# Early-fusion block: y hats clipped by ScalarE's int32 output, and attention scores as int16 in key-pair order

## The reference, cut to what matters

```
sampled = v00*(1-wy)*(1-wx) + v01*(1-wy)*wx + v10*wy*(1-wx) + v11*wy*wx

attn  = clip(round(q.k * sc / s), -128, 127)            # an integer times s
x_int = attn - max(attn);  x_int = max(x_int, 30*x0_int) # x0_int = floor(-0.6931/s)
qq    = floor(x_int / x0_int);  r = x_int - x0_int*qq
exp   = max(floor((r*(r + b_int) + c_int) * 2**(30 - qq)), 0)
ratio = round(sum(exp) / max(exp, 1))                    # rounded to a power of two
```

## Time and profile before

| what | value |
|---|---|
| median of 3 runs (lowest to highest) | 1015.75 us (1015.71 to 1016.1) |
| span of the profiled execution, first to last instruction | 1014.5 us |
| own time of the profiled execution | not given apart; the runs' median is 1.25 us above its span |
| PE busy | 880.8 us, 87% |
| DVE busy | 876.0 us, 86% |
| ACT busy | 779.8 us, 77% |
| POOL busy | 266.9 us, 26% |
| PE weight loads | 539.9 us, 53% |
| share of the 16 DMA engines | 24.5% |
| TensorE's granted clock, mean | 0.951 of full |

### The profile page before, as it was taken

The page is one execution under the profiler, slowest core; times in us unless marked ns, Lnnn a source line. Parts: engine busy times, 40 slices in busy tenths (PEclk is TensorE's granted clock), DMA queues, the critical chain, the costliest instruction groups (busy, mean ns, idle before and its releaser), DMA issues. The chain is left out here.

```text
span 1014.5 us, 18281 instructions
## 1 busy us (share of the span) xinstructions
PE 880.8 (87%) x5594; PEld 539.9 (53%) x5594; DVE 876.0 (86%) x1695; ACT 779.8 (77%) x1529; POOL 266.9 (26%) x248
## 2 busy tenths in 40 slices
PE   3568779999999999999999999999999999885757
PEld 1244436555565656565565656565556556453435
DVE  3964899998999899999999999999999999995960
ACT  2435587979888797979798988889797978785753
POOL 5210312315132313223041323141321414222120
PEclk9987769999999999999999999999999999998678
DMA  5110132221222232222213232323232232223030
GB/s 130 67 37 7 49 55 51 43 58 43 58 56 52 55 58 63 55 58 43 64 38 58 60 53 65 53 58 57 63 47 54 48 59 36 52 50 61 15 65 12
DMA packets 132628, 53.42 MB, mean 53 GB/s; under 512 B 105103, under 2 KB 131413, under 8 KB 132437
## 3 DMA queue, kind: packets, MB, share of 16 engines
q1 hardware_dynamic: 132532, 52.26, 24.5%
HBM read 19.75 MB, written 6.24 MB: 26 GB/s over the span
## 5 line engine op out<-in xcount | busy, mean ns | idle before, releaser
L563 POOL TENSOR_TENSOR ee_sb<-ee_sb,rs_sb 128x1020 f32<-128x1020 f32 x64 | 157.2, 2464 | 379.1 <-DVE rs_sb L1059 379.1
L1195 PE MATMUL bank<-hats_sb,ht_sb 127*96 127x400 f32 (+1 forms) x384 | 147.9, 522 | 1.7 <-DVE hats_sb L921 1.7
L1327 PE MATMUL bank<-w_out_sb,ge_sb 128*102 128x192 f32 x768 | 138.8, 331 | 10.9 <-DVE y_sb L1096 6.9
L1327 PEld LDWEIGHTS bank<-w_out_sb,ge_sb 128*102 128x102 f32 x768 | 120.3, 168 | 31.6 <-issue 17.8
L921 DVE TENSOR_TENSOR hats_sb<-hats_sb 126x1600 f32<-126x1600 f32 x64 | 127.2, 1987 | 0.7
L648 ACT ACTIVATE hats_sb<-bank 126x400 f32<-126x400 f32 (+1 forms) x256 | 108.2, 523 | 0.3 <-PE bank L1181 0.3
L727 ACT ACTIVATE a_sb<-scores,sc_sb 128x1020 f16<-128x1020 f32 x64 | 71.1, 1111 | 39.2 <-PE scores L1279 39.2
L1195 PEld LDWEIGHTS bank<-hats_sb,ht_sb 127*96 127x96 f32 (+1 forms) x384 | 58.7, 166 | 72.6 <-issue 69.3
L734 ACT ACTIVATE sq_sb<-rm_sb,sc_sb 128x1020 f32<-128x1020 f16 x64 | 73.5, 1148 | 18.2 <-DVE rm_sb L1031 18.0
L572 POOL TENSOR_TENSOR xshift_sb<-mv_sb,xshift_sb 102x4 f32<-102x4 f32 (+1 forms) x33 | 11.0, 333 | 279.9 <-DVE ve_sb L961 278.5
L1242 PE MATMUL bank<-xt_sb,w_in_sb 128*128 128x408 f32 (+1 forms) x204 | 82.0, 527 | 1.0 <-ACT xt_sb L667 1.0
(11 more groups left out here) (168 smaller groups left out, 1862.7 us busy)
## 6 DMA issues: line engine op xcount, KB each, us to landing
xc_sb<-x_col SPq DMA_DIRECT2D x32, 165.4 KB, 3.2
out<-y_sb SPq DMA_DIRECT2D x32, 153.0 KB
xa_sb<-txt SPq DMA_DIRECT2D x16, 231.0 KB
xr_sb<-txt SPq DMA_DIRECT2D x16, 231.0 KB
q_sb<-qb_sb SPq DMA_DIRECT2D x192, 12.8 KB, 1.9
samp_sb<-samp_sb SPq DMA_DIRECT2D x48, 50.0 KB, 1.9
tok_scratch<-tokb_sb SPq DMA_DIRECT2D x16, 75.0 KB
xa_sb<-tok_scratch SPq DMA_DIRECT2D x16, 75.0 KB
```

The costliest lines, as they stand in the source:

```text
L563: nc.gpsimd.tensor_tensor(EE[b][:], EE[b][:], RS[b][:].unsqueeze(2).to_broadcast([128, RT, TOK]), ALU.mult).then_inc(scaled_done, 1)
L1195: last = mm(dst, HT[0:rows, t.i, j, :], HATS[t.i][0:rows, 1 + j, :], start=(j == 0 and not odd), stop=(j == NCH - 2 and odd == 1))
L1327: last = mm(bank[t.banks[0]][0:TOK, 0:D], GE[:, f, t.i * TOK:(t.i + 1) * TOK], WOUT[:, f, :], start=(f == 0), stop=(f == FT - 1))
```

## The change

Two parts that share no data.

The y hats: ScalarE now writes the absolute y distance as int32, scaled by 2^31, so that every distance above 1 lands on the largest integer (`ONE_Y`); the x distance is scaled by 2^-31. `HAT` on DVE covers only the 400 x values, and `HATW` is a `scalar_tensor_tensor` that adds -2^31 to the integer y values and multiplies by x. `HAT` no longer waits for the y values; `HATW` does.

The scores: `A16`, `MX`, `M16`, `GQ` and `RM` become int16. PE writes the scores, and all softmax tiles up to `EE` keep them, in the order key pair, block, key of the pair (51 x 10 x 2). A new DVE stage `CLP` clips `A16` in place before `MAX`; `BND` is gone; `DST` becomes a plain `tensor_tensor` that subtracts the minimum less a lift from int16 values, so that results above 32767 stop there; the constants of `QQ`, `QQG`, `EP` and the square are changed to fit; `MX` and `RS` hold every value twice. Sums and the last minimum read by block across the key pairs, and ScalarE's Exp turns the order back to block, key.

```diff
-pe.LN2X.18 dve.MXB.53 act.LOG.15 dve.MAX.52 act.FFA.16 pe.HTT.5 dve.MXC.53 act.PR.15 dve.PREP0.0
-pe.SC.13 dve.MXB.52 act.FFN0.16 dve.DST.53 act.FFN1.16 pe.OFF.4 dve.BND.53 act.FFN2.16 sp.YO0.20
+pe.LN2X.18 dve.MXB.53 act.LOG.15 dve.CLP.52 dve.MAX.52 act.FFA.16 pe.HTT.5 dve.MXC.53 act.PR.15 dve.PREP0.0
+pe.SC.13 dve.MXB.52 act.FFN0.16 dve.DST.53 act.FFN1.16 pe.OFF.4 act.FFN2.16 sp.YO0.20
...
-                nc.scalar.activation(HATS[t.i][0:rows, 0, :], bank[t.banks[0]][0:rows, 0:SMP], ACT.Abs).then_inc(ax_done, 1)
+                nc.scalar.activation(HATS[t.i][0:rows, 0, :], bank[t.banks[0]][0:rows, 0:SMP], ACT.Abs,
+                                     scale=1.0 / ONE_Y).then_inc(ax_done, 1)
...
-                    nc.scalar.activation(HATS[t.i][0:rows, 1 + j, :], bank[t.banks[1]][0:rows, 0:SMP], ACT.Abs,
-                                         bias=float(-line)).then_inc(ay_done, 1)
+                    nc.scalar.activation(HATS[t.i][0:rows, 1 + j, :].bitcast(i32), bank[t.banks[1]][0:rows, 0:SMP], ACT.Abs,
+                                         scale=ONE_Y, bias=-line * ONE_Y).then_inc(ay_done, 1)
...
-                v.tensor_scalar(hat, hat, -1.0, 0.0, ALU.add, ALU.min).then_inc(hat_done, 1)
+                v.tensor_scalar(hat, hat, -1.0 / ONE_Y, 0.0, ALU.add, ALU.min).then_inc(hat_done, 1)   # hat: 400 columns, was 2000
...
-                v.tensor_tensor(hat[:, 1:, :], hat[:, 1:, :], hat[:, 0:1, :].to_broadcast([rows, NCH, SMP]),
-                                ALU.mult).then_inc(w_done, 1)
+                dve.wait_ge(ay_done, t.count(NCH, NCH))
+                v.scalar_tensor_tensor(hat[:, 1:, :], hat[:, 1:, :].bitcast(i32), -ONE_Y,
+                                       hat[:, 0:1, :].to_broadcast([rows, NCH, SMP]), ALU.add, ALU.mult).then_inc(w_done, 1)
...
-                nc.scalar.activation(A16[b][:].rearrange("p (j r) k -> p j (r k)", j=2), SCORES[:, :, 0:RC // 2], ACT.Identity,
-                                     scale=sc[:, SCORE:SCORE + 1], bias=MAGIC16).then_inc(a16_done, 1)
+                nc.scalar.activation(A16[b][:].rearrange("p (k j q) -> p j k q", j=2, q=RT),
+                                     SCORES[:, :, 0:RC // 2].rearrange("p j (k q) -> p j k q", q=RT), ACT.Identity,
+                                     scale=sc[:, SCORE:SCORE + 1], bias=EVEN_LIFT).then_inc(a16_done, 1)
...
-                nc.scalar.activation(RR[:], EE[b][:].rearrange("p h k -> p (h k)"), ACT.Exp, scale=-1.0).then_inc(rr_done, 1)
+                nc.scalar.activation(RR[:].rearrange("p (r k e) -> p r k e", k=KP, e=2), by_row(EE[b][:]), ACT.Exp,
+                                     scale=-1.0).then_inc(rr_done, 1)
...
+            def clip(t):
+                a = A16[t.i % 2][:]
+                dve.wait_ge(a16_done, t.count(1, 1))
+                v.tensor_scalar(a, a, EVEN_LIFT - 127.0, EVEN_LIFT + 128.0, ALU.max, ALU.min).then_inc(clip_done, 1)
...
-                v.tensor_reduce(MN[:], MB[:], AX.X, ALU.min).then_inc(min_done, 1)
+                v.tensor_reduce(MN[:], by_row(MB[:]), AX.XY, ALU.min).then_inc(min_done, 1)
...
-                v.tensor_scalar(MX[t.i % 2][:], MN[:], MAGIC16 + 128.0, MAGIC16 - 127.0, ALU.min, ALU.max).then_inc(mx_done, 1)
+                v.tensor_scalar(MX[t.i % 2][:], MN[:].unsqueeze(2).to_broadcast([128, RT, 2]), col(NLIFT), None,
+                                ALU.add).then_inc(mx_done, 1)
...
-                v.scalar_tensor_tensor(M16[b][:], A16[b][:], MAGIC16 + 128.0, MX[b][:].unsqueeze(2).to_broadcast([128, RT, TOK]),
-                                       ALU.min, ALU.subtract).then_inc(m_done, 1)
-            def bound(t):
-                v.tensor_scalar(M16[b][:], M16[b][:], 0.0, sc[:, G30:G30 + 1], ALU.max, ALU.min).then_inc(mc_done, 1)
+                v.tensor_tensor(M16[b][:].rearrange("p (k q) -> p k q", q=PAIRS), A16[b][:].rearrange("p (k q) -> p k q", q=PAIRS),
+                                over_key_pairs(MX[b][:]),
+                                ALU.subtract).then_inc(m_done, 1)
...
-                v.tensor_reduce(SS[b][:], EE[b][:], AX.X, ALU.add).then_inc(ss_done, 1)
+                v.tensor_reduce(SS[b][:], by_row(EE[b][:]), AX.XY, ALU.add).then_inc(ss_done, 1)
...
-                v.reciprocal(RS[b][:], SS[b][:]).then_inc(rs_done, 1)
+                v.reciprocal(RS[b][:], SS[b][:].unsqueeze(2).to_broadcast([128, RT, 2])).then_inc(rs_done, 1)
...
-                    dst = SCORES[:, r // (RT // 2), r % (RT // 2) * TOK:(r % (RT // 2) + 1) * TOK]
+                    dst = SCORES[:, r // RB, 0:KP * RT].rearrange("p (k r e) -> p r k e", r=RB, e=2)[:, r % RB, :, :]
```

More of the change, by code:

```diff
@@ L189, in build @@
     AX = mybir.AxisListType
[L190 removed]
+    f32, bf16, f16, i8, i16, u16, i32 = (
+            dt.float32, dt.bfloat16, dt.float16, dt.int8, dt.int16, dt.uint16, dt.int32)
     with ExitStack() as ctx:
```

105 lines of the change are left out of this document (57 added, 48 removed).

## The result

| | before | after |
|---|---|---|
| median (lowest to highest), 3 runs each | 1015.75 us (1015.71 to 1016.1) | 1055.49 us (1050.42 to 1058.19) |
| ratio, 95% interval | | 1.0411 [1.0377, 1.0445] |
| span of the profiled execution | 1014.5 us | 1048.3 us (a run of 1050.42 us) |
| DVE busy | 876.0 us | 849.8 us (forecast 794) |
| ACT busy | 779.8 us | 791.7 us |

The account below looks back on a forecast made before the run. It took the loop of PE and ScalarE, led by PE, as the bound, with DVE almost beside it. From 1015.75 us, 2.8 + 1.4 + 1.5 + 2.8 = 8.5 us off gave 1007 us, range 989 to 1017 (own 1000 to 1013).

Parts of the forecast that it names:

- The next work on DVE is late by what it saved: Where DVE waits for scores, `rr` or PE's feed-forward, nobody behind it is in a hurry; no cost taken.
- I take nothing for it since a pair stays together: Gapped pairs in `SUM`, `MXC`, ScalarE's Exp and GpSimd's pass cost nothing; bound 34 us in all for `SUM`.
- The sum on DVE: All priced DVE pieces together take 82 us off its 876 us busy, leaving near 794 us.
- DVE is full, yet almost beside the loop: In the even middle DVE is 94.88% busy, but only GpSimd's wait, 2.4 us, is on the loop through it.
- the 8.5 us of the forecast: Whole-kernel saving: 2.8 us GpSimd wait, 1.4 query transfer, 1.5 filling, 2.8 at the end.
- nothing comes through: Rival: PE's wait replaces GpSimd's, Exp or pair reads take some ns, the end gives 1 to 2 us; 1012.5 to 1017, chance 0.12.
- DVE as the pace: Rival: DVE's tight stream delays ScalarE at many small places, PE's middle idle halves; 994 us, 988 at best, chance 0.17.
- Score matmuls at half pace: Rival: PE writes gapped pairs slower, 704 matmuls at 41 ns more, 29 us; 1036 us, chance 0.07.
- `HATW` at two ticks: Rival: DVE's `HATW` takes 107 us more in all, DVE 901 us busy and pacing; at least 1041 us, chance 0.03.
- some ns: Size given to ScalarE's Exp or the pair reads in the rival of 1012.5 to 1017 us, chance 0.12.

Follow-up runs that it names:

- e9_rows: Changed kernel with DVE's subtraction writing distances row by row, so that everything behind it is laid out as before the change: 1024.87 us, 1.0135.
- e2_hats: Kernel before with the y hats' part of the change alone (`HAT` over 400 columns): 1023.1 us, 1.0112.
- e18_pairs_exp: Changed kernel with GpSimd's pass taken row by row and `FF2` ahead of `RCP`, ScalarE's Exp still in pairs: 1015.85 us, 1.0049.
- e17_pool_by_row_ff2: Changed kernel with GpSimd's pass taken row by row, ScalarE's Exp without gaps and `FF2` ahead of `RCP`: 1012.37 us, 1.0017.
- e3_scores: Changed kernel with the hats as before (`HAT` over 2000 columns): 1057.71 us, 1.0343.
- e7_scores_pr: Changed kernel with the hats as before and ScalarE's Exp without gaps (`PW` gathers the pairs): 1052.35 us, 1.0392.
- e11_pool_dose: Kernel before with GpSimd's pass in key pairs, using 20 repeated reciprocals of other rows: 1030.23 us, 1.0194.
- e8_pool: Changed kernel with ScalarE's Exp without gaps and GpSimd's pass over rows of 102, using other rows' reciprocals: 1009.39 us, 0.9958.
- e13_pool_by_row: Changed kernel with ScalarE's Exp without gaps and GpSimd's pass row by row over the pairs, one reciprocal a row: 1012.81 us, 1.0006.

## Why the prediction was wrong, by its own steps

**The account.** Three edits take the changed kernel back, one after the other: 1.0411, with `FF2` ahead of `RCP` 1.0188, with the pass row by row 1.0049, with the Exp without gaps 1.0017. By the medians the same four are 1.039, 1.026, 1.005 and 1.001. So the lost race is 1.3 to 2.2% (1.3% where undone in e9_rows and e2_hats), GpSimd's repeated reciprocals 1.4 to 2.1% (1.9% where tried alone), ScalarE's hops 0.3% (3 us; 0.7% alone). These are differences of ratios whose intervals are up to 0.8% either way.

**"The next work on DVE is late by what it saved", nobody being behind it in a hurry: failed.** DVE was in a hurry in one place, and being early there was what hurt. The prediction counted the 0.82 us that `HAT` saves without looking at what that `HAT` stood between: `RCP`, which releases another engine's long pass, and `EXP`, which shares ports with it. From the order and the trace of before it could be read: `EXP` started 0.16 us ahead of the pass only because `HAT` had filled the time in which ScalarE's square ended. The price is one `EXP` 2.2 us longer in each group, and behind it `FF2`, with PE waiting 1.6 us.

**"I take nothing for it since a pair stays together": failed for two of its four readers.** `SUM` and `MXC` cost nothing (1209 and 416 ns). ScalarE's Exp went from 1072 to 1262 ns. GpSimd's pass went from 1892 to 2339 ns at the least, and the only bound given was for `SUM`, which needed none. Both stand on the path of every picture, and the pass also holds off those DVE instructions that meet it.

**The sum on DVE: right as far as it went.** The priced pieces, after against before, are `HAT` -53.5, `DST` -33.6, `BND` -30.9, `CLP` +29.0, `MX` +2.1 and `RCP` +3.9 us, together -83 where the forecast had -82. In e18_pairs_exp, with race and pass mended, DVE is busy 794.3 us; the forecast said 794 (some luck is in the last digit: it has ten reciprocals and not twenty, and its `HATW` is shorter than before the change). The changed kernel has 849.8. The rows that stand for the 55.5 us between them: `EXP` 110.5 - 81.8 = 28.7, `HATW` on 126 partitions 75.3 - 62.7 = 12.6, `MXB` 31.9 - 24.8 = 7.1, the reciprocals 4, and the layer norm's variance step of four columns (L984) 6, less 3 on others. All but the reciprocals are DVE instructions that came out longer beside the pass and shorter without it; their wait is counted as busy time.

**"DVE is full, yet almost beside the loop": right, and more than was thought.** e17_pool_by_row_ff2 has 806.9 us busy on DVE, 69 less than before, and is not faster. Its stretch from 200 to 800 us, and ScalarE's waits there:

```profile
200.00:800.00 600.00, 567.95 (x3773) 350.20 (x3772) 521.75 (x1100) 519.02 (x1027) 154.42 (x152) 1.00 0.26 55
```

```profile
ACT a_sb L743 <- PE scores L1303: 22.1, 11, 2.9
ACT tokb_sb L678 <- PE bank L1234: 15.3, 11, 1.8
...
ACT ee_sb L757 <- POOL ee_sb L578: 3.2, 8, 0.5
```

PE is as busy as before (567.95 against 568.43), DVE 45.5 us less, and ScalarE waits for PE as in the earlier trace rows. Its wait for GpSimd did not go (3.2 against 2.4), so the 8.5 us of the forecast did not arrive even here. Mended, the change is the rival "nothing comes through".

**The rivals.** DVE as the pace: refuted by the same rows, since 45.5 us less on DVE made nothing faster. Score matmuls at half pace: 0.48 us for seven, refuted. `HATW` at two ticks: 1822 ns, refuted. The slow side came by a lost race that no rival had, and by pair reads that one rival named but took for "some ns".

**TensorE's clock in two experiments.** e3_scores and e7_scores_pr, with the hats as before and the pass in pairs, are at 1.034 and 1.039 with no long `EXP`, while the pass alone was worth 1.4 to 2.1% elsewhere. Part of the rest seems to be PE's clock. The first two rows are e7_scores_pr's middle and one us of it, the third its interpolation matmuls on 126 partitions:

```profile
200.00:800.00 600.00, 559.49 (x3557) 337.75 (x3558) 553.04 (x1031) 492.31 (x974) 161.38 (x140) 0.96 0.25 53
439.00:440.00 1.00, 1.00 (x2) 0.54 (x3) 0.99 (x4) 1.00 (x4) 0.00 (x0) 0.50 0.84 164
```

```profile
L1218 PE MATMUL bank<-hats_sb,ht_sb 126*96 126x400 f32 x192 | 93.5, 636 | 2.7 <-DVE hats_sb L942 2.7
```

The granted clock falls to 0.50 for some 3 us once in most groups, here after PE had been busy 0.45 of the us at 436 and 0.53 of that at 438, and the matmuls that stand there take 636 ns in the mean instead of 523. A mean of 0.96 over 600 us is 24 us at the full clock (an estimate from that row); before, the mean was 1.00. In e3_scores it is 0.98. PE is busy 909.4 us against 888.3 in e11_pool_dose, for the same number of matmuls: 21 us, where the two ratios lie 2.0%, 20 us, apart. It looks as if waits of PE cost a second time, through the clock. No run changes the clock alone, so this is read from the traces and not shown.

**What stays open.** DVE's busy time in those two (884 and 896 us) is above the kernel before and may add to it; that was not tested. e8_pool, which computes something else, is at 0.9958 with an interval that ends at 0.9997, and e13_pool_by_row, which keeps each reciprocal with its row, at 1.0006; the intervals overlap. No version that computes the same was measurably faster than the kernel before.

## What to carry to other kernels

Before an instruction is shortened or removed, see what its length was covering: look on its engine for the instruction behind it, and ask whether a long instruction of another engine, one that cannot run beside it, is released at nearly the same time. A busy time that rises on an instruction that was not touched is a wait in disguise; the least, median and most of its durations show it at once. When the layout of a tile changes, price each reader on each engine, since one engine's free hop is another's 20%.

## What the runs showed of the hardware

- DVE's `EXP` and GpSimd's pass never overlapped usefully: the one that lost ended about a whole length of the other later (3.45 = 2.35 + 1.10; 2.93 = 1.90 + 1.03; and the pass 2.81 instead of 1.89 where `EXP` was first, by 0.16 us). Between 0.03 us ahead and 0.05 us behind in the records, `EXP` lost; 0.05 us ahead (once, in e2_hats) and from 0.14 us on it won.
- ScalarE reading float32 pairs and writing 16-bit pairs with hops: 1262 ns for 1020 elements instead of 1072. DVE's sum over the same pairs: 1209, as contiguous. DVE's `PW` on 16-bit pairs: 618 instead of 422; its int16 subtraction 1081 instead of 687.
- GpSimd multiplying 1020 float32 values by 20 values repeated 51 times: at the least 2339 ns; by one value per row over the same pairs 2077 (e13_pool_by_row); by one value per contiguous row 1892 (before).
- PE writing float32 scores as pairs with gaps: 0.48 us for seven matmuls, as with 102 in a row (0.47).
- TensorE's granted clock of 0.50 for some 3 us in most groups of e7_scores_pr: a matmul of the interpolation takes 636 ns in the mean instead of 523.
- A subtraction of int16 with a repeated second input keeps the quick pace on DVE, 687 ns for 1020 elements; an int32 input beside a float32 one costs nothing, 1822 ns for 1600.
